# A decoder layer on one core: self attention on small tiles by head, its log1p polynomial on VectorE

## The reference, cut to what matters

```
x = layernorm(x + self_attention(x))            # the only stage that the change touches
x = layernorm(x + cross_attention(x, ctx))
x = layernorm(x + expert_ffn(x))

# self attention: B = 8 batches, T = 512 tokens, D = 256, H = 16 heads,
# key width S = 64, value width HD = 16, LV = 12 levels
Q, K, V = x Wq', x Wk', x Wv'
Lam     = softplus(Lp * (x Wdl'))               # (B, T, H, LV)
g       = -exp(A_log) * softplus(x Wdt' + dt_bias);  cg = cumsum(g over T)
W[t,s]  = (Q[t] . K[s]) / 8 * exp(cg[t] - cg[s]) * Lam[t, level(t, s)]     for s <= t
Y       = W V;   o = Y Wout' + x;   result = layernorm(o) * ln_g + ln_b
# level(t, s) = 0 if s == t, else 1 + floor(log2(s xor t)): 0 to 9 for 512 tokens
```

## Time and profile before

| | |
|---|---|
| median of 3 runs | 2115.41 us (2110.81 to 2115.58) |
| profiled execution | 2118.24 us, its span 2116.5 us |
| TensorE busy | 1808.8 us (85%), 11692 matmul instructions |
| VectorE busy | 1405.9 us (66%) |
| ScalarE busy | 985.6 us (47%) |
| GpSimd busy | 710.1 us (34%) |
| mean granted TensorE clock | 0.92 of full |

### The profile page before, as it was taken

One profiled execution on the slowest core, in us unless ns is written; L12 is line 12 of the kernel. 1 busy time (PEld: TensorE's weight loads), 2 busy tenths in 40 slices (PEclk: granted clock), 3 DMA queues, 4 the chain that ended last, 5 costly groups with the idle time before them and its releaser, 6 DMA issues. The chain is left out here.

```text
span 2116.5 us, 35526 instructions
## 1 busy us (share of the span) xinstructions
PE 1808.8 (85%) x11692; PEld 864.4 (41%) x11692; DVE 1405.9 (66%) x2834; ACT 985.6 (47%) x1415; POOL 710.1 (34%) x759
## 2 busy tenths in 40 slices
PE   3699889899898658999998989999989999985666
PEld 1355556555555422333333333343333433332224
DVE  4667877977878657686767857767778668831005
ACT  0355454555554412564554545545645456561113
POOL 1586686786774251303214013032040130000002
PEclk8799999999999967999999989999999999997775
DMA  5100000000000022110120111011201111145992
GB/s 180 70 21 1 20 20 0 20 10 10 20 10 1 1 88 66 42 49 22 47 67 8 62 45 46 30 39 47 65 8 61 43 46 49 79 190 204 422 386 93
DMA packets 64355, 142.26 MB, mean 67 GB/s; under 512 B 11376, under 2 KB 34448, under 8 KB 56048
## 3 DMA queue, kind: packets, MB, share of 16 engines
q1 hardware_dynamic: 59504, 136.34, 17.9%
q10 hardware_dynamic: 4736, 4.46, 0.6%
HBM read 97.64 MB, written 4.98 MB: 48 GB/s over the span
## 5 line engine op out<-in xcount | busy, mean ns | idle before, releaser
L1501 DVE TENSOR_REDUCE mx<-cpsV 128x1 f32<-128x512 f32 x1024 | 652.2, 685 | 240.5 <-PE cpsV L1204 233.2
L1405 ACT ACTIVATE w<-cpsA 128x1024 f32<-128x1024 f32 x512 | 496.3, 1021 | 385.8 <-PE cpsA L1272 385.6
L1204 PE MATMUL cpsV<-w 96*128 96x512 bf16 x1024 | 340.5, 404 | 64.6 <-DVE mx L1501 50.4
L1272 PE MATMUL cpsA<-w 99*128 99x512 bf16 x1024 | 280.0, 396 | 10.4 <-issue 9.8
L1226 PE MATMUL cacc<-w 128*32 128x512 f32 x2048 | 282.7, 618 | 0.4 <-ACT w L1405 0.4
L1062 POOL TENSOR_TENSOR w<-w,zero 128x1024 bf16<-128x1024 f32 x21 | 39.7, 1892 | 660.2 <-ACTq L1378 660.2
L1204 PEld LDWEIGHTS cpsV<-w 96*128 96x128 bf16 x1024 | 85.0, 100 | 381.1 <-DVE mx L1501 219.5
L1272 PEld LDWEIGHTS cpsA<-w 99*128 99x128 bf16 x1024 | 98.1, 100 | 139.8 <-issue 23.9
L596 ACT COPY QK<-psA 128x1024 f32<-128x1024 f32 x64 | 64.6, 1010 | 154.9 <-PE psA L462 154.8
L462 PE MATMUL psA<-xt,wq 128*128 128x512 f32 x256 | 126.7, 618 | 3.4 <-ACT VL L558 3.4
L462 PE MATMUL psA<-xt,wk 128*128 128x512 f32 x256 | 120.3, 592 | 0.0
(11 more groups left out here) (217 smaller groups left out, 2661.5 us busy)
## 6 DMA issues: line engine op xcount, KB each, us to landing
w<-in_w SPq DMA_DIRECT2D x64, 1024.0 KB, 16.4
w<-w SPq DMA_DIRECT2D x192, 128.0 KB, 2.3
w<-w SPq DMA_DIRECT2D x192, 64.0 KB, 2.0
w<-in_ctxT SPq DMA_DIRECT2D x8, 1024.0 KB, 5.2
pro_xt<-in_xT SPq DMA_DIRECT2D x8, 512.0 KB, 7.3
x_tok<-in_x SPq DMA_DIRECT2D x8, 512.0 KB, 9.1
xtv<-in_xT SPq DMA_DIRECT2D x8, 512.0 KB, 3.7
xt<-in_xT SPq DMA_DIRECT2D x8, 512.0 KB, 3.6
```

The costliest lines, as they stand in the source:

```text
L1204: nc.tensor.matmul(out, Qst[q // 2][0:ROWS, hh, g * P:(g + 1) * P], Kst[q // 2][0:ROWS, hh, half * BANK:(half + 1) * BANK], start=True, st ...
L1272: last = nc.tensor.matmul(out[:, n * T:(n + 1) * T], Kst[q // 2][0:ROWS + 3, hh, c * P:(c + 1) * P], Qst[q // 2][0:ROWS + 3, hh, :], start ...
L1405: nc.scalar.activation(Pr[:, (2 * s + pp) % 4, :], src, ACT.Exp, scale=CA_SCALE).then_inc(act_evac, 1)
L1501: nc.vector.tensor_reduce(mx[:, q % 2, row, k % 2:k % 2 + 1], full(m[k]), AX_X, ALU.max).then_inc(dve_evac, 1)
```

## The change

Only `self_attention` and the layout of two of its inputs change.

- Only the 10 levels that occur are computed (`LEVELS`), 640 instead of 768 columns.
- `vl` is split in `dl` (level logits, step 0) and two halves of V (`v` 1 at step 2 out of `xt`, for the same batch; `v` 0 at step 5 out of `xtv`, for the next). ScalarE writes V in place; GpSimd's copy of it is gone.
- Matmuls of `state`, `score`, `far` and `near` are cut by head and by token half or block: `state` 10 matmuls with 64 columns of weights, `score` 32 (64 rows, 32 columns, 32 moving), `far` 20 (64 rows, 64 columns, 16 to 64 moving), `near` 32 (32 rows, 32 columns, 16 moving). The zero-padded `KB`, `Wn`, `nearT` and the wide `WT` are gone. Scores come out with keys on the partitions, so that `WT` needs no transpose; instead `near_factors`, in two halves at steps 0 and 2, transposes the factor `LF` once a batch. `near` accumulates in the slot of `far`, and VectorE adds it to `Y` from there.
- In a step `states` comes first, then `qk`, `ktok`, `score`, `far` with `near`. `yT` is one job for both halves, at step 2. The tail has 4 steps instead of 5.
- `psV` has 2 slots of two banks instead of 4 of one.
- The polynomial is evaluated on VectorE alone (`POOL_POLY` is empty; `DVE_POLY`: terms 0 and 1 at step 3, 2 to 4 at step 4, 5 to 8 at step 6), `level_factors` follows at step 6 and the doubling (`block_factors`) at step 7.
- GpSimd adds `ln_b` to `x` (`add_lnb`, step 4) in place of VectorE's addition to `n1`.

The diff, cut to its core (nearly all removed lines are left out; they stand in the functions printed above):

```diff
+        return ["dl", ("v", 0)], v
+    for i in range(PAIRS if now else 4):
+        a += [("state", i)] * (sa_pair(section, i, 2) is not None)
+        a += [("qk", i)] * now
+        a += ["yT"] * (i == 2 and prev)
+        a += [("ktok", i)] * (sa_pair(section, i, 1) is not None)
+        a += ["dl"] * (i == 0 and nxt) + [("v", 1)] * (i == 2 and now) + [("v", 0)] * (i == 5 and nxt)
...
+        v += [("out", 0), ("out", 1)] * (i == 3 and prev)
...
+POOL_POLY = {}
+DVE_POLY = (-1, {3: (0, 2), 4: (2, 5), 6: (5, 9)})
...
+                    out = take_a(("state", i), after=before(i, "ktok"))
+                    pe.wait_ge(vp_ready, b * PAIRS + (i - 2 + 1))
+                    for n, (g, slot, count, column) in enumerate(STATES):
+                        for hh in range(2):
+                            r, c = slice(S * hh, S * hh + S), slice(HD * hh, HD * hh + HD)
+                            last = nc.tensor.matmul(out[r, HD * slot:HD * (slot + count)],
+                                                    Kt[:, g * P + S * hh:g * P + S * hh + S],
+                                                    VP[:, p % 2, g, column:column + count, c],
+                                                    start=(n == 0), stop=(n == len(STATES) - 1), skip_group_check=True)
...
+                    out = take_v(("score", i))
+                    by_token = take_a(("ktok", i), after=before(i, "qk"))
+                    for g in range(G):
+                        last = nc.tensor.transpose(by_token[:, g * P:(g + 1) * P],
+                                                   QK[:, p % 4, T + g * P:T + (g + 1) * P], sh.ident[:])
+                    last.then_inc(act_full, 1)
+                    for g in range(G):
+                        for j in range(P // BLK):
+                            t0 = g * P + j * BLK
+                            for hh in range(2):
+                                r, at = slice(S * hh, S * hh + S), BANK * hh + g * BLK
+                                last = nc.tensor.matmul(out[j * BLK:(j + 1) * BLK, at:at + BLK],
+                                                        QK[r, p % 4, T + t0:T + t0 + BLK], QK[r, p % 4, t0:t0 + BLK],
+                                                        start=True, stop=True)
+                    last.then_inc(dve_full, 1)
...
+                    for g in range(G):
+                        n = 4 if g < G - 1 else 3
+                        for half in range(2):
+                            t0 = g * P + 64 * half
+                            slots = slice(4 * g, 4 * g + n) if half else slice(4 * g, 4 * g + 3 * n - 2, 3)
+                            for hh in range(2):
+                                r, at = slice(S * hh, S * hh + S), BANK * hh + 4 * HD * g
+                                q = QK[r, p % 4, t0:t0 + 64]
+                                nc.tensor.matmul(out[64 * half:64 * half + 64, at:at + HD * n], q, Mst[r, slots, :],
+                                                 start=True, stop=True)
+                    for half in range(2):
+                        t0 = (G - 1) * P + 64 * half
+                        for hh in range(2):
+                            r, at = slice(S * hh, S * hh + S), BANK * hh + 4 * HD * (G - 1) + HD * LEVEL9
+                            nc.tensor.matmul(out[64 * half:64 * half + 64, at:at + HD], QK[r, p % 4, t0:t0 + 64],
+                                             Mst[r, 8, :], start=True, stop=True)
+                    for hh in range(2):
+                        for g in range(G):
+                            at = 4 * HD * G + 2 * HD * g + HD * hh
+                            for j in range(P // BLK):
+                                r = slice(j * BLK, (j + 1) * BLK)
+                                last = nc.tensor.matmul(out[r, at:at + HD], WT[r, p % 2, hh, g, :],
+                                                        V[r, g, HD * (2 * p + hh):HD * (2 * p + hh + 1)],
+                                                        start=True, stop=True)
...
+                        transpose_y()
+                    if two is not None:
+                        out = take_outputs(i, two)
+                    if one is not None:
+                        scores(i, one)
+                    if two is not None:
+                        outputs(out, two)
+                    if i == 0 and nxt:
+                        project_levels(b + 1)
+                    if i == 2 and now:
+                        project_values(1, xt)
+                    if i == 5 and nxt:
+                        project_values(0, xtv)
...
+                    if steps and sa_pair(sec, i, 2) is not None:
+                        nc.scalar.copy(Mst[:, 1:16, :], full(("state", i))[:, HD:16 * HD].rearrange("q (s c) -> q s c", c=HD)
+                                       ).then_inc(act_evac, 1)
...
+                        nc.scalar.copy(QK[:, i % 4, :], full(("qk", i))).then_inc(act_evac, 1)
+                    if i == 2 and prev:
+                        nc.scalar.copy(YT[:].rearrange("p k t -> p (k t)"), full("yT")).then_inc(act_evac, 1)
...
+                    for g, n in ((0, 5), (1, 4), (2, 4), (3, 3)):
...
+                def add_lnb():
+                    xb = sh.x[:, bass.ds((b - 1) * G, G), :]
+                    nc.gpsimd.tensor_tensor(xb, xb, lnb[:].unsqueeze(1).broadcast_to([P, G, D]), ALU.add
+                                            ).then_inc(lnb_added, 1)
...
+                def poly(first, last):
+                    uf, lamf = ul[:], lam[:].rearrange("p g h l -> p (g h l)")
+                    for n in range(first, last):
+                        if n == 0:
+                            dve.wait_ge(expz, bn + 1)
+                            nc.vector.tensor_scalar(lamf, uf, coefficients[0], None, ALU.mult)
+                        elif n == DVE_POLY[0]:
+                            dve.wait_ge(poly_ready, bn)
+                            nc.vector.tensor_tensor(lamf, lamf, uf, ALU.mult)
+                        else:
+                            nc.vector.scalar_tensor_tensor(out=lamf, in0=lamf, scalar=coefficients[n], in1=uf,
+                                                           op0=ALU.add, op1=ALU.mult)
+                        dve.drain()
...
+                def near_factors(half):
+                    hs = slice(8 * half, 8 * half + 8)
+                    double(5, 32 * half, 32 * half + 32)
+                    if half == 0:
+                        dve.wait_ge(decay_ready, b + 1)
+                    nc.vector.tensor_tensor(NEAR[:, hs].rearrange("p h g s -> p (h g s)"),
+                                            LF[:, hs].rearrange("p h g s -> p (h g s)"),
+                                            diff[:, hs].rearrange("p h g s -> p (h g s)"), ALU.mult)
+                    dve.drain()
+                    nc.vector.transpose(LF[:, hs], NEAR[:, hs])
...
+                        src = full(("score", i)).rearrange("p (h x) -> p h x", h=2)[:, :, 0:P]
+                        nc.vector.tensor_tensor(WT[:, p % 2].rearrange("p h g t -> p h (g t)"), src,
+                                                LF[:, 2 * p:2 * p + 2].rearrange("p h g t -> p h (g t)"), ALU.mult
+                                                ).then_inc(dve_evac, 1)
...
+                        nc.vector.tensor_tensor(yp, yp, src[:, 4 * HD * G:4 * HD * G + P].rearrange("p (g c) -> p g c", g=G),
+                                                ALU.add).then_inc(dve_evac, 1)
+                        if p == PAIRS - 1:
+                            dve.drain().then_inc(y_ready, 1)
...
+                    if i in DVE_POLY[1] and nxt:
+                        poly(*DVE_POLY[1][i])
+                    if i == 6 and nxt:
+                        level_factors()
                     if i == 7 and nxt:
-                        level_factors()
```

More of the change, by code:

```diff
@@ L42 @@
 EPS = 1e-5
-NV = D + H * LV
+HL = H * LEVELS
 BH = B * H
@@ L440, in transpose_y, with project_levels @@
[L440 to L442 removed]
+                def project_levels(bn):
+                    out = take_a("dl")
+                    pe.wait_ge(xv_loaded, bn * 16 + 16)
                     for g in range(G):
[L444 removed]
+                        at = g // 2 * BANK + g % 2 * HL
+                        for k in range(KD):
+                            last = nc.tensor.matmul(out[:, at:at + HL], xtv[:, k, g * P:(g + 1) * P], wdl[:, k, :],
+                                                    start=(k == 0), stop=(k == KD - 1))
@@ L445, in transpose_y, with project_values @@
                     last.then_inc(act_full, 1)
+                def project_values(half, x):
+                    out = take_a(("v", half))
+                    for g in range(G):
+                        for k in range(KD):
+                            last = nc.tensor.matmul(out[:, g * P:(g + 1) * P], x[:, k, g * P:(g + 1) * P],
```

(48 more changed lines are left out.)

403 lines of the change are left out of this document (141 added, 262 removed).

## The result

The changed kernel takes 2127.74 us (median; 2114.49 to 2138.16), the kernel before 2116.65 us beside it: the ratio is 1.0046, 95% interval 1.0028 to 1.0064. It is slower by about 10 us, where the prediction was 75 us faster. The profiled execution took 2122.48 us with a span of 2120.7 us.

The account below looks back on a forecast made before the run. TensorE was taken as the bound. A batch: 81.6 - 9.8 + 2.0 - 8 x 0.05 = 73.4 us; six middle batches -49, last -8, first -15, tail -3, together -75: 2040 us, range 1985 to 2105.

Parts of the forecast that it names:

- The reading of before: Self attention before the change: TensorE is the bound, and waits are 9.8 us of a batch's 81.6.
- The price of a small matmul: TensorE's score, far and near: 13.9 ns per instruction, taken from the old score row; small phases 3.64 us a step.
- Rival A: Score, far and near tiles cost more: at 24 ns each +109 us, 2149; chance 0.07 below break-even, 0.09 above.
- B: Rival: small tiles cost less, 7 ns each if issue allows; put at 1985 to 2000 us; chance 0.18.
- The waits that go: TensorE's waits for KB, Mst, VL and GpSimd's late VP disappear: all 9.8 us a batch.
- The new waits: TensorE behind four jobs a batch (dl, two v, yT) sharing two slots, and yT behind VectorE's Y: 2.0 us allowed.
- C: Rival: VectorE sets the pace in steps 5 to 1, up to 5 us a batch, 2065; 0.62 together with the forecast.
- Counting by the code: TensorE's five small phases of a step: 66 instructions become 188, while qk and ktok stay.
- D: Rival: granted clock falls to 1.2 GHz in small-tile phases and the qk behind them, over 200 us; chance 0.02.
- The first batch: Start of self attention, where TensorE stands until near at 94.58 waiting for VectorE: estimated 15 us shorter.

Follow-up runs that it names:

- e9: Changed kernel with TensorE's loop written out, far and near between the projection's two halves, and GpSimd's differences one step later: 2049.49 us.
- e1: Changed kernel with the loop over the six middle batches written out for TensorE alone: 2104.31 us.
- e6: Changed kernel with TensorE's loop written out and far and near placed between the projection's two halves, apart from scores: 2090.91 us.
- e15: The e9 kernel with SyncE's xtv load issued at step 5 instead of behind the other load at the batch's end: 2047.03 us.
- e5: Changed kernel with three quarters of the score and near matmuls left out in the six middle batches, TensorE's loop body 1871 instructions: 2059.22 us.

## Why the prediction was wrong

*The reading of before* held: TensorE the bound. The 9.8 us of waits a batch come from the strides of one step; the wait rows themselves give 35.6 / 5 = 7.1.

*The price of a small matmul* was too high. `score` is (0.76 - 0.199) / 63 = 8.9 ns from one to the next, `near` (0.73 - 0.180) / 63 = 8.7 ns, against 13.9 assumed and 24 feared; groups by line, 151.9 to 560.1 us:

```profile
L531 PE MATMUL psV<-V,WT 32*32 32x16 f32 x2368 | 29.5, 180 | 20.9 <-issue 20.9
L495 PE MATMUL psV<-QK 64*32 64x32 f32 x2368 | 28.0, 199 | 0.0
```

The small phases take 0.72 + 0.69 + 0.70 + 0.66 = 2.8 us a step instead of the forecast 3.64 (before 3.69): -7 us a batch. Rival A is out, B's premise was right. The start-to-start floor of 25 ns that the prediction cited from the Trainium skill does not hold for tiles on different strips.

*The waits that go* went: `KB`, `VL` and the late `VP` of the polynomial. *The new waits* are VP 12.7 / 4.7 = 2.7, `Mst` 0.9 and `QK` 0.2 a batch, 3.9 instead of 2.0: the allowance did not see that `differences` stands in front of a VP.

*VectorE* was no bound (C out): 92 us of its idle time stand in front of `WT`, waiting for scores.

**The step that failed is the sum's silent term: "Counting by the code" made 188 instructions of 66 a step, and priced them by TensorE's time alone.** Their number has a cost of its own once the loop body doesn't stay: 3407 instructions against 1427. Per batch, "issue" is 43.4 / 4.7 = 9.2 us. And **D, priced as a clock that falls for small tiles, came in by another door**: behind the stretches the granted clock is at 1.2 GHz for a while instead of 2.4 (0.50 from 402.87 to 406 us, 0.90 in the mean). A `qk` matmul averages (89.5 + 72.1) / 299 = 0.54 us of busy time after and (78.3 + 75.2) / 320 = 0.48 before, +3.9 us a batch, and by their groups' averages `dl` (3.9 us a batch instead of the forecast 2.3) and `out` (25.5 / 5 = 5.1 instead of 19.9 / 5 = 4.0) 2.7 more. The rows:

```profile
L463 PE MATMUL psA<-xt,wq 128*128 128x512 f32 x151 | 89.5, 722 | 4.7 <-ACT Mst L634 4.4
L463 PE MATMUL psA<-xt,wk 128*128 128x512 f32 x148 | 72.1, 610 | 0.0
```

```profile
L462 PE MATMUL psA<-xt,wq 128*128 128x512 f32 x160 | 78.3, 612 | 2.8 <-ACT VL L558 2.8
L462 PE MATMUL psA<-xt,wk 128*128 128x512 f32 x160 | 75.2, 592 | 0.0
```

From the forecast: 73.4 + 9.2 (fetch) + 6.6 (clock) + 1.9 (waits) - 7 (tiles) = 84.1 of the measured 87.1; a `qk` stride of 3.53 instead of 3.43 us is 0.8 more, and 2.2 are not accounted for.

With the fetches hidden and `differences` moved, a batch takes 72.5 us and self attention ends at 673.4 us, 75 before the 748.0: the forecast's figures, for a kernel that it did not describe, and in part by errors of opposite sign (cheaper tiles, waits for `Kt` and `xt` that it had not named).

*The first batch* did not give its 15 us: the first `xt` load behind it comes at 138.7 instead of 141.7 us. TensorE still waits for VectorE there. The profile calls it "issue", but no packet lies in the 4.35 us, and the wait ends with VectorE's `WT`; in e9 the profile names that `WT` for 4.39 us. Behind it TensorE runs at a granted clock of 0.50 until 95 us. Of fetches there are 1.44 us in front of 103.56 and 1.41 in front of 133.23.

```profile
86.42 0.42 DVE L888 TENSOR_TENSOR WT<-psV,LF 128x256 f32<-128x256 f32 x1
86.95 1.09 PE L487 MATMUL psA<-ident,QK 128*128 128x128 f32 x4 [4.35 <-issue]
```

**Open.** In the kernels whose loop is written out and whose tiles are small (e1, e6, e9, e15) the rest is 1376 to 1380 us, in the changed kernel 1346 to 1348. In one window of cross attention and the experts, from 60 us behind its start, the same work (busy VectorE 785 and 786 us) takes 1094 us after and 1122 us in e9, with clocks of 0.96 and 0.94:

```profile
832.00:1926.00 1094.00, 1011.00 (x5307) 386.73 (x5306) 784.99 (x1547) 590.69 (x635) 204.25 (x112) 0.96 0.16 56
```

```profile
733.00:1855.00 1122.00, 1025.10 (x5307) 394.36 (x5306) 785.92 (x1547) 590.68 (x635) 204.29 (x112) 0.94 0.16 55
```

Of the 99.0 us by which e9's self attention is shorter than the changed kernel's, 28.4 go back behind it. The clock is one difference that shows; the other is that TensorE is idle for 97 us instead of 83. Why either is so is not settled. Also untried: where between 1683 and 1871 the body falls out, whether its position in the program counts beside its length, and what sets the stretch at a branch between 2.7 and 6.0 us.

## What to carry to other kernels

Count the instructions of an engine's loop body before cutting its matmuls smaller, weight loads included: here 1683 stayed and 1871 did not. If it doesn't stay, write the loop out, and put long matmuls between the dense runs so that each block arrives while they work; writing it out alone left half of the stalls (22.7 of 43.4 us). And when work leaves one engine's queue, look at what else stands in front of the same wait: the polynomial was worth 81 to 95 us of self attention, the next item 14 to 28 (758.6 against 772.4 and 786.3).

## What the hardware showed unexpectedly

- A taken branch back to code that has to be fetched cost 4.5 to 6.0 us in the changed kernel and its variants, 5.2 to 5.8 us still with three quarters of `score` and `near` left out (e5), and 2.7 to 3.1 us in the old tiling; a block of dense code without a branch mostly 1.4 to 2.0 us; a block of thin code nothing.
- Naming the branch ahead cut that stretch to 3.0 to 3.4 us; in the whole no gain could be told.
- Small float32 matmuls on strips of rows and columns: 8.7 to 8.9 ns from one to the next.
- The same program behind self attention took 1346 to 1380 us, by execution and by what ran ahead of it.
